# A Mamba block in slots: who makes the last sum of the softplus, DVE or POOL

## The reference, cut to what matters

```python
xb = silu(conv(x_br))
Bm, Cm = xb @ W_b, xb @ W_c
delta = softplus(xb @ W_delta + b_delta)
A_bar = exp(delta[..., None] * A)
Bx = delta[..., None] * Bm[:, :, None, :] * xb[..., None]
h = A_bar[t] * h + Bx[t]          # for t in order
y[t] = sum(h * Cm[t][:, None, :], axis=-1)
```

## Time and profile before

| What | Value |
|---|---|
| time, median of 3 runs | 2808.11 us (2806.92 to 2808.42) |
| profiled execution, its own time | 2811.04 us |
| its span from first to last instruction | 2808.1 us |
| DVE busy | 2330.2 us, 83% |
| PE busy | 2345.5 us, 84% |
| ACT busy | 1707.3 us, 61% |
| POOL busy | 1679.8 us, 60% |
| mean granted TensorE clock | 0.922 |

### The profile page before, as it was taken

How to read it: one execution, slowest core, us unless ns; L and a number is a source line. 1 busy time by engine, 2 the same in 40 slices (tenths; PEclk the granted TensorE clock), 3 DMA queues, 4 the chain that set the end, 5 groups by cost and what they waited for, 6 DMA issues and landing times. The chain is left out here.

```text
span 2808.1 us, 34215 instructions
## 1 busy us (share of the span) xinstructions
PE 2345.5 (84%) x11488; PEld 1623.8 (58%) x11520; DVE 2330.2 (83%) x2358; ACT 1707.3 (61%) x3314; POOL 1679.8 (60%) x1993
## 2 busy tenths in 40 slices
PE   7878888888888888888887888888888684999997
PEld 5656666575757575756565757566666231444443
DVE  2489898989898989898988989898989554788886
ACT  2556666676757575757576667566666334655554
POOL 0267776767676767776776767677767440222221
PEclk8879999999999999999999999999998896999999
DMA  4101020202020101101010202020102632111110
GB/s 176 68 1 68 9 72 5 72 5 76 2 75 16 61 26 51 51 26 61 16 69 8 69 8 69 9 68 9 64 5 94 236 117 76 61 56 67 56 61 23
DMA packets 47435, 151.73 MB, mean 54 GB/s; under 512 B 7973, under 2 KB 8869, under 8 KB 44206
## 3 DMA queue, kind: packets, MB, share of 16 engines
q1 hardware_dynamic: 47278, 149.76, 15.1%
HBM read 132.37 MB, written 17.37 MB: 53 GB/s over the span
## 5 line engine op out<-in xcount | busy, mean ns | idle before, releaser
L450 POOL TENSOR_TENSOR ring<-ring,Cbc 128x512 f32<-128x512 f32 x1024 | 1286.9, 1278 | 45.4 <-POOL carry L443 1.7
L846 DVE TENSOR_TENSOR_SCAN ring<-a_ps,ring 128x1024 f32<-128x1024 f32 x512 | 1165.3, 2278 | 77.9 <-ACT a_ps L662 77.9
L662 ACT ACTIVATE a_ps<-delta,nA 128x255 f32<-128x255 f32 x2048 | 852.3, 466 | 419.6 <-DVE ring L846 418.6
L1043 PE MATMUL yT_ps<-ident,ring 128*128 128x128 f32 x4096 | 610.1, 292 | 178.4 <-POOL ring L450 174.6
L838 DVE TENSOR_TENSOR ring<-u_ps,Bbc 128x1024 f32<-128x1024 f32 x512 | 621.1, 1213 | 98.4 <-PE yT_ps L1043 91.7
L1043 PEld LDWEIGHTS yT_ps<-ident,ring 128*128 128x128 f32 x4096 | 495.4, 149 | 289.1 <-POOL ring L450 253.3
L443 POOL TENSOR_TENSOR carry<-ring,half 128x4 f32<-128x4 f32 x512 | 149.6, 292 | 564.8 <-DVE ring L846 562.2
L1009 PE MATMUL work<-xb,big 128*128 128x256 f32 x2048 | 480.1, 388 | 0.0
L1009 PEld LDWEIGHTS work<-xb,big 128*128 128x128 f32 x2048 | 390.3, 196 | 50.7 <-issue 0.4
L1025 PE MATMUL work<-Wout,xb 128*128 128x512 f32 x512 | 246.4, 618 | 0.0
L978 PE MATMUL work<-y0s,big 128*128 128x256 f32 x1024 | 233.1, 380 | 0.0
(11 more groups left out here) (195 smaller groups left out, 2630.2 us busy)
## 6 DMA issues: line engine op xcount, KB each, us to landing
Bbc<-bc_rows SPq DMA_DIRECT2D x64, 512.0 KB, 4.6
Cbc<-bc_rows SPq DMA_DIRECT2D x64, 512.0 KB, 3.7
xT<-in_xT SPq DMA_DIRECT2D x16, 514.0 KB, 3.6
x_rows<-x2row SPq DMA_DIRECT2D x32, 256.0 KB, 2.0
xp<-x_rows SPq DMA_DIRECT2D x32, 256.0 KB, 2.7
xx<-in_x SPq DMA_DIRECT2D x32, 256.0 KB, 2.9
out_rows<-orow SPq DMA_DIRECT2D x32, 256.0 KB, 2.0
delta<-in_c_w SPq DMA_DIRECT2D x6, 1024.0 KB, 5.6
```

Of the source, the lines that this page charges most:

```text
L450: nc.gpsimd.tensor_tensor(hp, hp, Cbc[:, G * g + GP * c:G * g + GP * c + GP, :], ALU.mult)\
L662: r = nc.scalar.activation(a_ps[q % 2][:, i, 1:T], delta[:, par, dt, 1:T], ACT.Exp, scale=nA[:, dt, s:s + 1])
L846: dve.tensor_tensor_scan(ring[:, q % RING, :, :].rearrange("p g t -> p (g t)"), a_ps[q % 2][:, :, :].rearrange("p g t -> p (g t)"), ring[: ...
L1043: r = pe.matmul(yT_ps[:, tt, :], ring[:, q % RING, i, P * tt:P * tt + P], ident[:, :], is_transpose=True, start=False, stop=(g == NG - 1 a ...
```

## The change

The two sums leave DVE's plans and become `delta_sum` in POOL's list. POOL makes the second half's sum at the start of its slot 6, the first half's at the start of its slot 26. Both stand ahead of the wait for that slot's scan. The operation, its operands and its semaphore stay the same.

```diff
+SUMS = (26, 6)
@@ POOL
+            def delta_sum(pair, b, bp):
+
+                for j in (2 * pair, 2 * pair + 1):
+                    pool.wait_ge(free[BANK[f"DL{j}"]], jobs_before(f"DL{j}", b - 1) + 1)
+                pool.wait_ge(s_dln, 2 * b + pair + 1)
+                d = delta[:, bp, 4 * pair:4 * pair + 4, :].rearrange("p a b -> p (a b)")
+                nc.gpsimd.tensor_tensor(d, d, ln_full[:, :], ALU.add).then_inc(s_delta, 1)
+
             def step(k, par, front, back, scan):
                 for q in range(NQ):
                     dt, g = q // NG, q % NG
+                    if scan and q == SUMS[1]:
+                        delta_sum(1, k, par)
+                    if front and q == SUMS[0]:
+                        delta_sum(0, k + 1, 1 - par)
@@ DVE
-                def dmax(pair, late):
-                    for j in (2 * pair, 2 * pair + 1):
-                        dve.wait_ge(free[BANK[f"DL{j}"]], jobs_before(f"DL{j}", k - 1 if late else k) + 1)
-                    dve.wait_ge(s_dln, 2 * (k if late else n) + pair + 1)
-                    d = delta[:, par if late else fp, 4 * pair:4 * pair + 4, :].rearrange("p a b -> p (a b)")
-                    dve.tensor_tensor(d, d, ln_full[:, :], ALU.add).then_inc(s_delta, 1)
-
@@
-                             13: [keep_y0], 27: [lambda: dmax(0, False)]}
-                scan_plan = {7: [lambda: dmax(1, True)]}
+                             13: [keep_y0]}
```

More of the change, by code:

```diff
@@ L860, in step @@
                             dve.memset(a_ps[i][:, :, 0:1], 0.0).then_inc(s_aclr, 1)
-                    for job in (scan_plan.get(q, []) if scan else []):
-                        job()
                     for job in (next_plan.get(q, []) if front else []):
```

## The result

The changed kernel takes 2786.72 us (median of four runs, 2783.35 to 2787.16), the kernel before 2807.52 (four runs). The ratio is 0.9921 with an interval of 0.9909 to 0.9934, so the change gains 20.8 us. 2790 was forecast. The profiled execution took 2786.70 us, its span is 2784.9.

What follows compares the result with a forecast made beforehand. DVE was taken to pace most slots, PE and ACT slots 12 to 18. From 2808.1, 15 blocks at 0.9 (13.5) less ends of 1.3 and 1.2 gave 2797.1; the clock's 6.8 more gave 2790.3, range 2782 to 2804.

Steps and rivals of the forecast that it cites:

- Slot 7 gains nothing: Slot 7: DVE's delta times xb product is held until POOL's 2.5 us sum ends; 0.3 us lost a block.
- Slot 27 gains: Slots 27 to 31: scan 27 starts 0.9 us earlier, right behind ACT; by slot 31 the gain is 1.2 us.
- the 1.1 to 1.3 that the prediction named as a sign: Slot 31: DVE's delta times xb product was to take 1.1 to 1.3 us instead of 1.43.
- the path's term: Each of 15 blocks: 1.2 us gained by slot 31 less 0.3 lost in slot 7, 0.9 a block, 13.5 in all.
- The ends: Before block 0 the unhidden sum loses 1.3 us; in the last block held DVE work loses 1.2.
- The clock: PE's restart in slot 18: blocks all turn short after some three, 0.57 us each, 12 x 0.57 = 6.8 more.
- The short kind: The shorter of two alternating block kinds before, 134.27 against 135.39 us; its clock returns 3.0 us after PE's restart.
- (b): Rival: block kinds stay mixed half and half, so no clock gain; 2797.1 us, chance 0.27.
- (c): Rival: block pairs stay at 269.65 us, each block's gain spent at low clock; 2810.6 or 2808, chance 0.08.
- (f): Rival: low clock reaches slots 12 to 15, costing 1.5 us there, blocks 0.6 longer; 2819.6, chance 0.08.
- (d): Rival: slot 7's delta times xb product isn't held by the sum; 34.8 us gained, 2774.6, chance 0.06.
- (e): Rival: slot 31's product meets a multiplication's start; gain there 0.5, 0.2 a block, 2807.6, chance 0.07.

Runs made afterwards that it cites:

- two-instruction kernel: Changed kernel with each POOL sum made as two instructions of 128x512 instead of one of 128x1024, no filling: 2792.95 us, ratio 0.9950.
- slot 8 kernel: Changed kernel with the second half's sum in POOL's slot 8 instead of 6, no filling: 2831.24 us, ratio 1.0079.
- filled changed kernel: Changed kernel with 52 transposes of zeros added to PE's list in slot 18, without effect on the output: 2784.82 us, ratio 0.9916.
- three fillings: 90 transposes of zeros a block in PE's pauses (slots 10 and 11, 18, 27): kernel before 2790.54 us, changed kernel 2767.92 us.

## Why the prediction was right

**Slot 7 gains nothing.** Right, and the reason too: L823 is held to the end of POOL's instruction. The step that gave a loss of 0.3 us took 2.5 us as the sum's length; it is 2.34 to 2.37, and the loss 0.07. What no row of before had, a hold by one instruction of over 1.28 us, showed as the Trainium skill's rule has it (SBUF — State Buffer, section "Who interferes with whom"): L823, issued 1.01 us after the sum, waited to its end. The section's words on the whole instruction stand at VectorE's two-port modes; here a plain product with both inputs in SBUF was held so. Cutting that instruction in two shortened the hold by 1.07 us.

**Slot 27 gains.** Right in each link: the scan behind ACT, no wait of POOL for the logarithm, L823 of slot 31 in the first multiplication instead of the second. 1.2 was forecast for both together and 1.46 measured; POOL was 0.23 us further on than assumed, mostly because its sum is shorter, so L823 took 0.84 there and not the 1.1 to 1.3 that the prediction named as a sign. So the path's term was 0.9 us a block and measures 1.39, in undisturbed blocks 1.35 to 1.37. It is the term that was sized too small.

**The ends.** The sum before block 0 costs 1.2 us, not 1.3: ACT's logarithm to L823 takes 2.55 instead of 1.39. The other 0.6 by which block 0 starts later was there before that: 0.43 of it already at the first L734, 23 us into the program. The last block loses 0.8 in slot 7, not 1.2: L809 is held for 2.1 us, but L813 goes no slower for it.

**The clock.** The forecast that all blocks become of one kind, with the clock back soon after PE's restart, came true within three blocks. Its size was taken from the wrong base. The short kind, 134.27, was treated as free of the clock; undisturbed it would be 133.45. The clock cost 1.4 us a block before and still costs 1.0. So it gave 0.35 us a block, not 0.57. And the block of now isn't the short block of before: that one had its clock back 3.0 us after the restart and was low again around slots 27 to 29, this one has it back after 3.5 and isn't low there. The prediction looked at the restart alone. The two mis-sized terms, 0.5 too little for the path and 0.2 too much for the clock, cancel by about half; the rest is about the 3.3 us between 2790 and 2786.7. That the number came out so near is in part luck.

**The rivals.** (b), mixed kinds, didn't happen in this kernel and did in the one with two instructions. (c) and (f) were given 0.08 each as possible fates of this change. They are real fates of close neighbours: the two-instruction kernel gave back all it saved and, by the medians, 6 us more, and the slot 8 kernel went to the wrong side through the stretch that (f) names, with a longer low stretch after the restart beside it. (f)'s price of 1.5 us for a low stretch there was right: 133.62 against 132.10 in the filled changed kernel. And the kernel before does pay it once, in the step of block 14, where the prediction says that no block does. What I couldn't do before the result, and can't now, is tell from the rows which neighbour gets which pattern. That part of the forecast was right by a judgement, not by a derivation. (d) is refuted by 1.89 us, (e) by 0.84.

Left open is what decides between an execution of 2785.7 and three near 2793 of one and the same kernel.

## What to carry to other kernels

A DVE product with both inputs in SBUF and a long POOL instruction that meet run one behind the other: 1.89 us instead of 0.69 here, while L844, with one input in PSUM, kept its 1.2 us. So when work is moved to POOL, look which DVE instruction stands beside its new place, and cut the POOL instruction or move it by a slot or two. In a loop like this one, where PE's clock takes two levels within each block, the time alone is no measure of one edit. Fill PE's pauses for a moment, in both kernels, and compare them so: unfilled, the slot 8 kernel is 23 us slower than the kernel before; both filled, it is 34 us faster (2756.13 against 2790.54). And the best kernel of this study, 2755.88 us with three fillings and sums in two instructions, is 1.9% below the kernel before.

## What the runs showed of the hardware

Useless work made the kernel faster. 90 transposes of zeros a block raised the granted clock from 0.93 to 0.97 between 400 and 1900 us (from 0.95 to 0.98 in the two-instruction kernel) and took 15 us off the kernel before, 19 off the changed one and 37 off the two-instruction one. The low level costs time in three places of this block: at the start of slots 12 to 15, behind PE's restart, and around slots 27 to 29. Elsewhere it costs nothing: the blocks with three fillings still have it around slot 4 and in some blocks around slots 8 or 31 to 1, and differ by 0.2 us at most. What is left of it in the changed kernel, 1.0 us a block, is the stretch behind the restart, since its other one, in slots 11 and 12, ends 1.3 us before PE's first products. This loop fell into several fixed patterns: 133.1, pairs of 135.4 and 134.3, threes of 136.2, 135.6 and 134.4, and 136.5 were all held for many blocks by kernels whose undisturbed blocks differ by some 2 us.
